# The input gate's tanh stays in its PSUM bank, and the vector engine reads it there half by half

## The chip, the cores and the metric

The kernel runs on one NeuronCore of a Trainium2 chip. The metric is the device time of one execution in microseconds (us); three executions of the kernel before gave 147.38, 147.51 and 147.60, a median of 147.51. Engines are named as the profile names them: PE is the tensor engine's matmuls and PEld its weight loads, DVE the vector engine, ACT the scalar engine, POOL the GpSimd engine, SP the engine that only issues transfers. A differing time of about 0.2% (0.3 us) is the least that such runs tell from no change.

## What is computed

The input x has 16 sequences of 256 tokens with 128 features, 4096 tokens in all. It is layer-normalised to xn, and the output is x + attn(xn) + ffn(xn).

```python
# attn: a gated linear recurrence along each sequence
xc  = causal_depthwise_conv(xn, 4 taps)
r   = sigmoid(xc @ W_r.T + b_r);   i = sigmoid(xc @ W_i.T + b_i)
a   = sigmoid(log_a) ** (8 * r)
h_t = a_t * h_(t-1) + sqrt(1 - a_t^2) * (i_t * xc_t)
attn = rmsnorm(h @ W_out.T) * gamma
# ffn: each token goes to one of 8 experts, at most 512 tokens per expert
e   = argmax(softmax(xn @ Wr));  y = relu(xn @ W1[e]) @ W2[e] * prob[e]
```

A sigmoid is had from a tanh: sigmoid(z) = 0.5 (tanh(z/2) + 1). So `gated` computes (tanh + 1) * xc, and the factor 0.5 is carried in the scale.

## The kernel before, in words

Everything is written out by hand: each engine has its own list of instructions, which it works off in order, and engines wait for one another on counting semaphores (`wait_ge(sem, n)` passes once the count has reached n).

**Stages.** First x is loaded and normalised, the router picks an expert per token, and a table of row numbers per expert is built. Then comes the long middle stage: eight experts one after the other, with the recurrence's work placed between them. At the end the rows of y are loaded back, scaled and added, and the output is stored.

**One expert e** on PE is `turn` (four transposes of the gathered tokens), `up` (12 matmuls into three banks `hbank`) and `down` (16 matmuls, each of which the profile counts twice, x32 on L624). ACT copies the transposed tokens (`columns`, L778), applies the ReLU (`relu`, L786, four times) and rounds the next weights (`lead`, L730). DVE computes the remainders of these roundings (`columns_rest`, L1028, `weights_rest`, L1003) and copies the result out of PSUM (`evict`, L1068; for expert 6 in two halves, L1075; for expert 7 in four quarters, L1080).

**POOL** issues the indirect transfers, one instruction for 128 rows: `gather` (L405) fetches an expert's tokens in four instructions, `scatter` (L417) writes its results in four. Its order is gathers 0 to 3, then scatter 0, gather 4, scatter 1, gather 5, scatter 2, gather 6, scatter 3, gather 7, scatters 4 to 7. A scatter waits for the copies of `evict` on the semaphore `y_done`; the first two instructions of scatter 6 wait for the first half of expert 6, and each instruction of scatter 7 for its own quarter. SP waits for all scatters before it loads the rows of y back (L339).

**The gates.** The tokens of the recurrence are cut into four chunks (c = 0 to 3) of 1024 columns, each of two halves of 512. For a chunk there are four gate halves, i = 0 to 3: i = 0, 1 are the recurrence gate r for the two halves, i = 2, 3 the input gate i. `gate_half(c, i)` on PE (L553 for chunk 0, L561 to L563 for the others) writes into one of two PSUM banks, `gate[i % 2]`; `gate_half` on ACT (L754) applies tanh to it and writes SBUF: `dec` for i = 0, 1 and `inp` for i = 2, 3. ACT's tanh counts up `gate_free`, and PE may write a bank again once the tanh of two gate halves before has read it. So ACT alone frees the gate banks.

**The gated input.** `gated(c)` on DVE (L1045) waits for all four tanhs of the chunk, then computes `inp = (inp + 1) * xc` for both halves from SBUF and counts `gated_done` once. `recur` (L1057, L1061) multiplies it by the scale and runs the recurrence; `project` on PE (L640) multiplies its result by W_out and reuses the gate banks.

**Where these stand in each engine's list.** The plans `PE_AT`, `ACT_AT`, `DVE_AT`, `DVE_LATE` and so on (L294 to L303) place the stages by expert. On PE `gates1` comes behind `down(0)` and ahead of `up(1)`, `gates2` behind `down(1)` and `gates3` behind `down(2)`. On DVE the order from the point of interest is: convolution taps of chunk 2, `columns_rest(1)`, `gated0`, clip 0, `evict(0)`, taps of chunk 3, `split2`, `weights_rest(2)`, `columns_rest(2)`, `gated1`, `evict(1)`, `split3`, clip 1, `gated2`, and so on; `gated3` follows `evict(2)`. On ACT `gates1` is followed by `relu(1)`, `lead2`, `decay1` with its square, and `columns(2)`.

Of the kernel before, what the change touches and what calls it, by code (L numbers as in the profile page):

```python
# [9 lines left out]
ALU = mybir.AluOpType  # L10
# [8 lines left out]
C = 4  # L19
# [27 lines left out]
def rglru_moe_kernel(nc, x, params, gamma, weights, xn_rows, y_rows, out):  # L47
# [17 lines left out]
    with ExitStack() as ctx:  # L65
# [6 lines left out]
        def sem(name):  # L72
            return ctx.enter_context(nc.semaphore(name))
# [163 lines left out]
        clip_done = sem("clip_done")  # L237
        scale_done = sem("scale_done")
        gated_done = sem("gated_done")
        input_done = sem("input_done")  # L240
# [197 lines left out]
        def _(pe):  # L438
# [105 lines left out]
            def gate_half(c, i):  # L544
                n = 4 * c + i
                convolved(pe, 2 * c + i % 2)
                if n >= 2:
                    pe.wait_ge(gate_free, n - 1)
                else:
                    pe.wait_ge(xnT_done, NH)  # L550
# [78 lines left out]
            def project(n):  # L629
# [3 lines left out]
                if n >= 3:  # L633
                    pe.wait_ge(sum_done, n - 2)
                else:
                    pe.wait_ge(gate_free, 4 * C)
                    pe.wait_ge(dump_done, 1)
# [34 lines left out]
        def _(act):  # L672
# [74 lines left out]
            def gate_half(c, i):  # L747
                n = 4 * c + i
                dst, bias = (dec, 0) if i < 2 else (inp, 1)
                act.wait_ge(gate_mm, n + 1)  # L750
                if c == 2 and i == 2:
                    act.wait_ge(low_done, len(LOW_STARTS))
                o = c * TC + (i % 2) * HT
                a(dst[:, o:o + HT], gate[n % 2][:, :], ACT.Tanh, bias=half_b[:, bias:bias + 1],  # L754
                  scale=0.5).then_inc(gate_free, 1)

# [9 lines left out]
            def decay(c):  # L766
                cols = slice(c * TC, (c + 1) * TC)
                if c == 0:
                    act.wait_ge(coef, 6)
                    act.wait_ge(zero_out, 16 * C)  # L770
                act.wait_ge(gate_free, 4 * c + 2)
                a(dec[:, cols], dec[:, cols], ACT.Exp, bias=lna[:, 5:6], scale=lna[:, 5:6]).then_inc(decay_done, 1)
# [81 lines left out]
        def _(dve):  # L854
# [185 lines left out]
            def gated(c):  # L1040
                dve.wait_ge(gate_free, 4 * c + 4)
                convolved(dve, 2 * c)
                convolved(dve, 2 * c + 1)
                for half in halves(c):
                    last = v.scalar_tensor_tensor(inp[:, half], inp[:, half], 1.0, xc[:, half], ALU.add, ALU.mult)  # L1045
                last.then_inc(gated_done, 1)

            def recur(n):
                cols = slice(n * HT, (n + 1) * HT)
                given = obank[IN_OBANK[n]][:, :]  # L1050
                dve.wait_ge(scale_done, n // 2 + 1)
                dve.wait_ge(gated_done, n // 2 + 1)
                if n >= 1:
# [151 lines left out]
```

## Time and profile before

| | |
|---|---|
| median of three executions | 147.51 us |
| span of the profiled execution, first to last instruction | 128.8 us |
| what lies around the span (147.51 less 128.8) | 18.7 us |
| PE busy | 106.2 us, 82% of the span |
| DVE busy | 101.8 us, 79% |
| ACT busy | 99.6 us, 77% |
| POOL busy | 84.6 us, 66% |
| granted TensorE clock, mean over the span | 0.958 of full speed |

The span is that of one profiled execution; no time of its own is given for it beside the span, so the 18.7 us between it and the median are taken as the part outside the first and last instruction. Times in the rows below are microseconds from the span's start. A row of a timeline merges neighbouring instructions of one line (xN); its bracket tells idle time of the engine just before and what ended it. "issue" in the chain of waits, or as a releaser, is time for which the profile shows no one that was waited for. L12 is line 12 of the kernel before.

### The profile page before, as it was taken

Reading aid. Unit: us, or ns where it says so; the run is one execution under the profiler, and the core shown is the slowest. Engines: PE = TensorE matmul, PEld = TensorE weight load, DVE = VectorE, ACT = ScalarE, POOL = GpSimd, SP = SyncE. Lnnn points to the kernel's source line nnn. Section 1 sums busy time; section 2 is a strip of 40 time slices with the busy share of each in tenths; the row PEclk is TensorE's granted clock in tenths of the full one; section 3 lists DMA queues with packets and bytes.
Section 4 is the critical chain, followed back from the end, with each engine's and each line's share of the span. In section 5 each row is a group of like instructions: output and inputs, shape, how many; then the busy total and the mean of one; then the engine's idle time right before and its main releaser. Section 6 shows DMA issues by size and latency. Waiting matters only on the chain.

```text
span 128.8 us, 2229 instructions
## 1 busy us (share of the span) xinstructions
PE 106.2 (82%) x711; PEld 89.9 (70%) x711; DVE 101.8 (79%) x238; ACT 99.6 (77%) x219; POOL 84.6 (66%) x109
## 2 busy tenths in 40 slices
PE   3999999999799999999999997999997999700000
PEld 3999976672379779789879987898697899600000
DVE  5398998999699999979614489999999975973690
ACT  3299792888589589789689999999999799823560
POOL 8987774078788787778777877888787878700000
PEclk9999999999999999999999999999999999998555
DMA  2966964892456365312611711111110111149995
GB/s 85 383 247 173 405 244 173 318 380 66 103 169 181 80 209 139 118 53 56 209 41 41 219 51 41 61 37 41 52 57 25 60 43 61 41 108 302 325 372 215
DMA packets 8234, 19.27 MB, mean 150 GB/s; under 512 B 1689, under 2 KB 1945, under 8 KB 8224
## 3 DMA queue, kind: packets, MB, share of 16 engines
q1 hardware_dynamic: 5424, 13.70, 31.5%
q0 software_dynamic: 2080, 4.19, 11.2%
q10 hardware_dynamic: 720, 1.25, 2.6%
q8 instruction: 5, 0.08, 0.2%
q14 instruction: 5, 0.04, 0.1%
HBM read 10.82 MB, written 8.39 MB: 149 GB/s over the span
## 4 chain that ended last, share of the span: by engine, by line
PE 60%; DVE 9%; DMA 8%; ACT 8%; issue 5%; POOL 4%; POOLq 1%; SPq 1%; DVEq 0%; ACTq 0%
PE bank L624 17%; PE bank L609 6%; PE bank L611 6%; PE bank L610 6%; DMA dec<-y_rows 4%; PE bank L640 4%; PE bank L453 3%; PE bank L561 3%; PE bank L442 3%; POOL xn_tok L405 3%; DMA xn_tok<-xn_rows,idx_in 2%; ACT xc L796 2%; PE bank L594 2%; PE bank L563 2%; PE bank L562 2%
## 5 line engine op out<-in xcount | busy, mean ns | idle before, releaser
L405 POOL DMA_INDIRECT xn_tok<-xn_rows,idx_in x32 | 33.7, 1054 | 14.4 <-issue 9.4
L417 POOL DMA_INDIRECT y_rows<-xn_tok,idx_out x32 | 33.5, 1047 | 9.7 <-issue 9.1
L624 PE MATMUL bank<-w_raw,h_sb 128*128 128x128 f32 x256 | 29.9, 275 | 0.0
L624 PEld LDWEIGHTS bank<-w_raw,h_sb 128*128 128x128 f32 x256 | 29.2, 192 | 0.0
L786 ACT ACTIVATE h_sb<-bank 128x512 f32<-128x512 f32 x32 | 18.8, 598 | 2.5 <-PE bank L611 0.6
L609 PE MATMUL bank<-xg_hi,w_hi 128*128 128x512 f32 x32 | 13.2, 412 | 0.0
L611 PE MATMUL bank<-xg_hi,w_lo 128*128 128x512 f32 x32 | 12.6, 393 | 0.0
L610 PE MATMUL bank<-xg_lo,w_hi 128*128 128x512 f32 x32 | 12.5, 391 | 0.0
L1021 DVE SCALAR_TENSOR_TENSOR xc<-xnT,par,xc 128x1020 f32<-128x1020 f32 (+2 forms) x9 | 11.5, 1277 | 0.3
L640 PE MATMUL bank<-par,xc 128*128 128x128 f32 x64 | 8.8, 280 | 2.2 <-ACT xc L796 1.3
L1061 DVE TENSOR_TENSOR_SCAN xnT<-dec,bank 128x256 f32<-128x256 f32 x16 | 10.1, 674 | 0.3
L640 PEld LDWEIGHTS bank<-par,xc 128*128 128x128 f32 x64 | 8.0, 191 | 3.1 <-ACT xc L796 1.6
L805 ACT ACTIVATE sq<-bank 128x128 f32<-128x128 f32 x32 | 8.9, 277 | 1.0 <-PE bank L640 0.3
L836 ACT ACTIVATE dec<-dec,prob 128x128 f32<-128x128 f32 x16 | 5.1, 389 | 5.8 <-DMA dec<-y_rows 5.8
L380 POOL TENSOR_SCALAR xn_tok<-x_tok,rstd,nmr 128x128 f32<-128x128 f32 x15 | 7.7, 529 | 2.8 <-DVE nmr L884 2.8
L453 PE MATMUL bank<-w_router,dec 128*128 128x128 f32 x64 | 8.6, 278 | 0.4 <-ACT dec L694 0.3
L754 ACT ACTIVATE dec<-bank,half_b 128x512 f32<-128x512 f32 x8 | 5.5, 689 | 4.2 <-PE bank L563 3.2
L453 PEld LDWEIGHTS bank<-w_router,dec 128*128 128x128 f32 x64 | 7.8, 192 | 0.9 <-ACT dec L694 0.5
L1028 DVE TENSOR_TENSOR xg_lo<-bank,xg_hi 128x512 fp32r<-128x512 f32 x8 | 5.5, 688 | 3.5 <-ACT xg_hi L778 3.3
L796 ACT ACTIVATE xc<-xnT 128x512 f32<-128x512 f32 x8 | 8.2, 1105 | 0.0
L609 PEld LDWEIGHTS bank<-xg_hi,w_hi 128*128 128x128 f32 x32 | 6.0, 188 | 2.5 <-DVE xg_lo L1028 0.9
L1045 DVE SCALAR_TENSOR_TENSOR inp<-inp,xc 128x512 f32<-128x512 f32 x8 | 5.2, 689 | 2.9 <-ACT inp L754 2.9
(143 smaller groups left out, 243.2 us busy)
## 6 DMA issues: line engine op xcount, KB each, us to landing
w_raw<-in_weights SPq DMA_DIRECT2D x8, 512.0 KB, 3.9
y_rows<-sca SPq DMA_DIRECT2D x4, 512.0 KB, 5.9
dec<-y_rows SPq DMA_DIRECT2D x8, 256.0 KB, 5.7
x_tok<-in_x SPq DMA_DIRECT2D x3, 512.0 KB, 5.9
xn_rows<-xn_tok SPq DMA_DIRECT2D x3, 512.0 KB, 3.6
out<-dec SPq DMA_DIRECT2D x4, 256.0 KB, 3.1
out<-dec ACTq DMA_DIRECT2D x4, 256.0 KB, 2.9
x_tok<-in_x SPq DMA_DIRECT2D x2, 256.0 KB, 3.5
```

What stands on the lines that cost most here:

```text
L405: g.indirect_dma_start(gathered[:, s * D:(s + 1) * D], None, xn_rows, bass.IndirectOffsetOnAxis(ap=idx_in[:, s:s + 1], axis=0)).then_inc(g ...
L417: g.indirect_dma_start(y_rows, bass.IndirectOffsetOnAxis(ap=idx_out[:, s:s + 1], axis=0), gathered[:, s * D:(s + 1) * D], None, bounds_che ...
L453: last = mm((bank[6], bank[2])[t // PT][:, o:o + D], xT[:, t * P:(t + 1) * P], w_router[:, :], start=True, stop=True)
L609: mm(b, w_hi[:, e % 2, w], xg_hi[:, :], start=True, stop=False)
L610: mm(b, w_hi[:, e % 2, w], xg_lo[:, :], start=False, stop=False)
L611: mm(b, w_lo[:, e % 2, w], xg_hi[:, :], start=False, stop=True).then_inc(h_mm, 1)
L624: last = mm(tile_of(e, s), h_sb[:, k * CAP + s * P:k * CAP + (s + 1) * P], w_raw[:, e, F + k * D:F + (k + 1) * D], start=(k == 0), stop=(k ...
L640: last = mm(obank[n % 3][:, i * D:(i + 1) * D], ordered[:, t * P:(t + 1) * P], par[:, WO_T:WO_T + D], start=True, stop=True)
L786: a(h_sb[:, k * CAP:(k + 1) * CAP], hbank[n % 3][:, :], ACT.Relu).then_inc(h_done, 1)
L796: a(ordered[:, cols].rearrange("d (i p) -> d p i", i=RUN), hs[:, cols].rearrange("d (p i) -> d p i", i=RUN), ACT.Copy).then_inc(order_done, 1)
L1021: ins = v.scalar_tensor_tensor(dst[:, :, back:], src[:, :, 0:L - back], par[:, k:k + 1], dst[:, :, back:], ALU.mult, ALU.add)
L1061: last = v.tensor_tensor_scan(hs[:, o:o + L], dec[:, o:o + L], given[:, s * L:(s + 1) * L], 0.0, ALU.mult, ALU.add)
```

## The change

The semaphore `tanh_done` is new. ACT's tanh of an input-gate half (i = 2, 3) now writes back into the PSUM bank it reads, instead of into `inp`, and counts `tanh_done` instead of `gate_free`. `gated(c)` on DVE now takes the halves one at a time: it waits for that half's tanh, reads it from the PSUM bank `gate[i]`, writes `inp` in SBUF, and counts `gated_done` per half. PE's rule for a gate bank follows: for i = 2, 3 it waits, as before, for the tanh of i - 2 of the same chunk; for i = 0, 1 of a chunk after the first it now waits for `gated` of the chunk before, on that half. `project` waits for both counts, and ACT's wait for `low_done` (the SBUF space of `inp` was shared with a table of the router) is gone, because DVE itself writes `inp` now. The order of the stages on every engine, the number of matmuls, tanhs and DVE operations, and all transfers are as before.

```diff
--- before.py
+++ after.py
@@ -236,6 +236,7 @@
         square_done = sem("square_done")
         clip_done = sem("clip_done")
         scale_done = sem("scale_done")
+        tanh_done = sem("tanh_done")
         gated_done = sem("gated_done")
         input_done = sem("input_done")
         scan_done = sem("scan_done")
@@ -544,8 +545,10 @@
             def gate_half(c, i):
                 n = 4 * c + i
                 convolved(pe, 2 * c + i % 2)
-                if n >= 2:
-                    pe.wait_ge(gate_free, n - 1)
+                if i >= 2:
+                    pe.wait_ge(gate_free, 2 * c + i - 1)
+                elif c >= 1:
+                    pe.wait_ge(gated_done, 2 * (c - 1) + i + 1)
                 else:
                     pe.wait_ge(xnT_done, NH)
                 if c == 0:
@@ -633,7 +636,8 @@
                 if n >= 3:
                     pe.wait_ge(sum_done, n - 2)
                 else:
-                    pe.wait_ge(gate_free, 4 * C)
+                    pe.wait_ge(gate_free, 2 * C)
+                    pe.wait_ge(gated_done, 2 * C)
                     pe.wait_ge(dump_done, 1)
                 for i in range(4):
                     t = 4 * n + i
@@ -746,13 +750,13 @@
 
             def gate_half(c, i):
                 n = 4 * c + i
-                dst, bias = (dec, 0) if i < 2 else (inp, 1)
                 act.wait_ge(gate_mm, n + 1)
-                if c == 2 and i == 2:
-                    act.wait_ge(low_done, len(LOW_STARTS))
-                o = c * TC + (i % 2) * HT
-                a(dst[:, o:o + HT], gate[n % 2][:, :], ACT.Tanh, bias=half_b[:, bias:bias + 1],
-                  scale=0.5).then_inc(gate_free, 1)
+                if i < 2:
+                    o = c * TC + i * HT
+                    a(dec[:, o:o + HT], gate[n % 2][:, :], ACT.Tanh, bias=half_b[:, 0:1], scale=0.5).then_inc(gate_free, 1)
+                else:
+                    a(gate[n % 2][:, :], gate[n % 2][:, :], ACT.Tanh, bias=half_b[:, 1:2],
+                      scale=0.5).then_inc(tanh_done, 1)
 
             def gates(c):
                 for i in range(4):
@@ -768,7 +772,7 @@
                 if c == 0:
                     act.wait_ge(coef, 6)
                     act.wait_ge(zero_out, 16 * C)
-                act.wait_ge(gate_free, 4 * c + 2)
+                act.wait_ge(gate_free, 2 * c + 2)
                 a(dec[:, cols], dec[:, cols], ACT.Exp, bias=lna[:, 5:6], scale=lna[:, 5:6]).then_inc(decay_done, 1)
                 if c < 2:
                     square(c)
@@ -1038,18 +1042,17 @@
                 return [slice(n * HT, (n + 1) * HT) for n in (2 * c, 2 * c + 1)]
 
             def gated(c):
-                dve.wait_ge(gate_free, 4 * c + 4)
-                convolved(dve, 2 * c)
-                convolved(dve, 2 * c + 1)
-                for half in halves(c):
-                    last = v.scalar_tensor_tensor(inp[:, half], inp[:, half], 1.0, xc[:, half], ALU.add, ALU.mult)
-                last.then_inc(gated_done, 1)
+                for i, half in enumerate(halves(c)):
+                    convolved(dve, 2 * c + i)
+                    dve.wait_ge(tanh_done, 2 * c + i + 1)
+                    v.scalar_tensor_tensor(inp[:, half], gate[i][:, :], 1.0, xc[:, half], ALU.add,
+                                           ALU.mult).then_inc(gated_done, 1)
 
             def recur(n):
                 cols = slice(n * HT, (n + 1) * HT)
                 given = obank[IN_OBANK[n]][:, :]
                 dve.wait_ge(scale_done, n // 2 + 1)
-                dve.wait_ge(gated_done, n // 2 + 1)
+                dve.wait_ge(gated_done, 2 * C)
                 if n >= 1:
                     dve.wait_ge(scan_done, n)
                 if n == 6:
```

## Rows read from the trace of the kernel before

**Rows 1.** The page's chain that ended last, by engine:
```profile
PE 60%; DVE 9%; DMA 8%; ACT 8%; issue 5%; POOL 4%; POOLq 1%; SPq 1%; DVEq 0%; ACTq 0%
```

**Rows 2.** The chain of waits, 42 to 82 us: start, duration, engine and line:
```profile
43.26 0.23 PE bank L561
...
44.78 0.47 PE bank L561
...
53.15 0.23 PE bank L561
...
63.05 0.24 PE bank L561
...
75.55 0.25 PE bank L611
...
75.82 0.02 ACT h_sb L786
```

**Rows 3.** POOL's timeline: start, duration, line, operation, idle time before and releaser:
```profile
25.89 0.98 POOL L405 DMA_INDIRECT xn_tok<-xn_rows,idx_in  x1 [4.93 <-DVE idx_out L986]
...
57.97 1.29 POOL L417 DMA_INDIRECT y_rows<-xn_tok,idx_out  x1 [0.30 <-issue]
...
102.41 0.97 POOL L417 DMA_INDIRECT y_rows<-xn_tok,idx_out  x1 [0.31 <-issue]
...
107.52 0.97 POOL L417 DMA_INDIRECT y_rows<-xn_tok,idx_out  x1 [0.30 <-issue]
108.80 0.97 POOL L417 DMA_INDIRECT y_rows<-xn_tok,idx_out  x1 [0.30 <-DVE xn_tok L1080]
...
111.35 0.97 POOL L417 DMA_INDIRECT y_rows<-xn_tok,idx_out  x1 [0.30 <-issue]
```

**Rows 4.** Who waited for whom, POOL: total us, times, longest:
```profile
POOL y_rows L417 <- issue: 9.1, 30, 0.3
```

**Rows 5.** The line of expert 7's copies: duration min/median/max, first and last start:
```profile
L1080 DVE COPY xn_tok<-bank x4: 291/292/292, 105.5 to 108.2; 128x128 f32<-128x128 f32 x4
```

**Rows 6.** DVE's timeline around the couplings to POOL and to ACT:
```profile
24.91 0.19 DVE L985 TENSOR_SCALAR idx_in<-bank 128x32 int32<-128x32 f32 x1 [0.19 <-PE bank L481]
...
79.43 0.69 DVE L1028 TENSOR_TENSOR xg_lo<-bank,xg_hi 128x512 fp32r<-128x512 f32 x1 [0.30 <-ACT xg_hi L778]
...
100.50 0.74 DVE L1075 COPY xn_tok<-bank 128x256 f32<-128x256 f32 x2
...
116.65 1.14 DVE L1168 SCALAR_TENSOR_TENSOR dec<-dec,prob,x_tok 128x128 f32<-128x128 f32 x4 [1.63 <-issue]
```

**Rows 7.** Busy time by stretch: length, PE, PEld, DVE, ACT, POOL, PEclk, DMA share, GB/s:
```profile
79.40:100.50 21.10, 19.53 (x140) 17.41 (x138) 20.18 (x38) 20.14 (x56) 16.53 (x16) 1.00 0.15 45
```

**Rows 8.** DVE's timeline, 43 to 60 us:
```profile
43.09 1.32 DVE L1045 SCALAR_TENSOR_TENSOR inp<-inp,xc 128x512 f32<-128x512 f32 x2
...
53.03 0.69 DVE L1028 TENSOR_TENSOR xg_lo<-bank,xg_hi 128x512 fp32r<-128x512 f32 x1
53.63 1.28 DVE L1045 SCALAR_TENSOR_TENSOR inp<-inp,xc 128x512 f32<-128x512 f32 x2
54.84 0.68 DVE L1068 COPY xn_tok<-bank 128x512 f32<-128x512 f32 x1
...
58.91 1.28 DVE L1045 SCALAR_TENSOR_TENSOR inp<-inp,xc 128x512 f32<-128x512 f32 x2
```

**Rows 9.** ACT's timeline, 43 to 53 us:
```profile
43.99 0.69 ACT L754 ACTIVATE dec<-bank,half_b 128x512 f32<-128x512 f32 x1 [1.31 <-PE bank L563]
...
47.13 2.64 ACT L786 ACTIVATE h_sb<-bank 128x512 f32<-128x512 f32 x4
...
52.42 0.58 ACT L778 ACTIVATE xg_hi<-bank 128x512 fp32r<-128x512 f32 x1
```

**Rows 10.** PE's timeline: the last matmul of `up(1)`:
```profile
48.75 0.39 PE L611 MATMUL bank<-xg_hi,w_lo 128*128 128x512 f32 x1
```

**Rows 11.** DVE's groups by form: count, busy us, mean ns, idle before:
```profile
L1003 DVE TENSOR_TENSOR w_lo<-w_raw,w_hi 128x512 fp32r<-128x512 f32 x8 | 5.5, 689 | 1.9 <-ACT w_hi L730 1.9
L1028 DVE TENSOR_TENSOR xg_lo<-bank,xg_hi 128x512 fp32r<-128x512 f32 x8 | 5.5, 688 | 3.5 <-ACT xg_hi L778 3.3
L1045 DVE SCALAR_TENSOR_TENSOR inp<-inp,xc 128x512 f32<-128x512 f32 x8 | 5.2, 689 | 2.9 <-ACT inp L754 2.9
```

## The prediction

> **What bounds the kernel now.** I read the chain of waits first. By engine it is 60% PE [rows 1], and in its pieces the tensor engine stands in an unbroken string from 43 to 75.8 us: gates, `up`, `turn`, `down`, gates again [rows 2]. At 75.82 it passes to ACT, whose fourth ReLU of expert 4 starts 0.02 us after PE's last `up` matmul ended at 75.80. So in this stretch a microsecond lost on PE is a microsecond lost for PE, ACT and DVE alike.
>
> Then I looked at the end of the chain, because a chain is only as true as its joints. It goes through DVE's last copy of expert 7 to the POOL instruction at 108.80, which the profile puts down to that copy line [rows 3]. But the gap before it is 0.30 us, and 30 of the 32 scatter instructions show the same gap with nobody waited for [rows 4]. The instruction at 108.80 is the second of scatter 7 and needs only the second copy. The four copies start between 105.5 and 108.2 [rows 5], some 0.9 apart, so that one was done near 106.7, two us earlier. POOL was not waiting; it was working off a backlog. From 25.89, when the first gather started, to 112.3 its 64 instructions follow one another with gaps of 0.3 [rows 3, 4]: the train on POOL is a second bound beside PE, and at the end it is the later one. The reader is to take from this that PE's stretch has slack against POOL, and how much is a subtraction:
>
> - scatter 6, first instruction, starts at 102.41 [rows 3]; the first half of `evict(6)` starts at 100.50, and two take 0.74 with the second starting behind the first, so the first ends near 100.91 (100.50 + 0.41) [rows 6];
> - scatter 7, first: 107.52 against a copy that ends at 105.8 [rows 3, 5];
> - scatter 7, last: 111.35 against 108.5;
> - scatter 1: 57.97 against 55.52 (54.84 + 0.68) [rows 3, 8].
>
> What POOL needs between a copy's end and its own start I call L. Its bounds: 0.03, if the constant 0.30 can be spent ahead of the wait (0.03 is what DVE took after ACT's `columns` ended at 79.40 [rows 6]); 0.79, from the index table's copy at 24.91 + 0.19 to the first gather at 25.89 [rows 3, 6]. I take 0.33, the gap of the sixty-odd others plus 0.03. Scatter 6 is the tightest: 102.41 - 0.33 - 100.91 = 1.17 us of slack.
>
> **The change, part by part.** *Two new waits on PE.* Before `gates1` PE needed only ACT's tanhs of chunk 0, done long before; now its first half needs the first half of `gated0`, which DVE starts at 43.09, behind the taps and `columns_rest(1)`. Two halves take 1.32 in all, each 0.68 to 0.69 [rows 8, 11], so the first ends at 43.77 and the second at 44.41. From a release to the matmul PE takes 0.10: the tanh of 43.99 + 0.69 = 44.68 released the matmul at 44.78, and after such a halt the first matmul counts 0.47 in the chain instead of 0.23 [rows 2, 9]. So PE starts at 43.87 and is through its first matmul at 44.34, where it was through at 43.49 (43.26 + 0.23): 0.85 lost. The second half follows under cover: its input is free at 44.41, and PE wants it near 44.8. Behind the halted matmul stand the rest of `gates1`, `up(1)`, `turn(2)`, `down(1)`, and ACT's tanhs and ReLUs wait for those.
>
> Before `gates2` the same wait is on `gated1`. This one starts at 53.63 behind `columns_rest(2)`, which started at 53.03, just after ACT's `columns(2)` ended at 52.42 + 0.58 = 53.00 [rows 8, 9]. Does DVE's side move with PE's? ACT gets to `columns(2)` in order, behind four ReLUs from 47.13 to 49.77, the last of which starts near 49.17; the last `up(1)` matmul ends at 48.75 + 0.39 = 49.14 [rows 9, 10]. So ACT runs at PE's pace, and `gated1` is late by the same 0.85: the first half ends at 53.63 + 0.68 + 0.85 = 55.16, PE starts at 55.26 and is through its first matmul at 55.73, against 53.38 before [rows 2]. That is 2.35 in all: 0.85 from the first wait, 1.50 from the second. Before `gates3` nothing is lost: `gated2` starts at 58.91 and its first half is done by 59.60, PE comes at 63.05 [rows 2, 8], and both move by the same 2.35.
>
> *The tanh written to PSUM.* No ACT write to PSUM stands in the trace. What it could save or cost lies on ACT between the third gate half and `relu`, and there ACT waits for PE matmul by matmul, as shown; a tenth of a microsecond either way per tanh is absorbed within the four ReLUs. I take zero.
>
> *The DVE read from PSUM.* `columns_rest` reads PSUM and takes 688 ns for 128x512, `weights_rest` with SBUF inputs 689, `gated` 689 [rows 11]. I take no difference; the spread of these rows, some 0.02 per half, is the bound, counted once in each of the two waits. Beside this stands a rule that speaks against the change: the Trainium skill (Perfetto Trace Analysis, Optimizing Scalar/DVE Operations) gives a DVE operation an access overhead of about 60 ns on SBUF and about 125 ns on PSUM. By that each of the two waits would grow by an estimated 0.065 us and the forecast below by 0.13, to 148.82; the rows show no such difference.
>
> *Half by half.* `gated3` is the one place where DVE waited for a tanh, 2.9 us once [rows 11]. Its first half can now start one tanh earlier, 0.69; but DVE waits 1.9 for the weights of the next `weights_rest` right after it [rows 11], so this is worth nothing. `recur` now waits for all of `gated`, which stands ahead of it on the same engine anyway. The removed wait for the router's table and the added one in `project` have been satisfied for tens of microseconds. No transfer moves in any queue's order.
>
> *How much reaches the end.* The 2.35 passes over PE and ACT to 79.43, where DVE starts `columns_rest(5)` when ACT releases it, and from there DVE is busy 20.18 of 21.10 us up to `evict(6)` [rows 6, 7], with no wait for another engine that is longer than its own pipeline gaps. So the first half of `evict(6)` ends at 100.91 + 2.35 = 103.26, and scatter 6 starts at 103.59 instead of 102.41: 1.18 late. The train then runs on as before: scatter 7's first would come at 108.70, and its copy is ready at 105.8 + 2.35 + 0.33 = 108.48. The last stage hangs on the last scatter; its DVE work had 1.63 idle before 116.65 [rows 6], more than the 1.17 by which DVE is now later than POOL. So of 2.35 lost on PE, POOL's backlog hides 1.17 and 1.18 reach the end. Against the profiled execution: 128.8 + 1.18 = 129.98; what lies around the span stays, so 147.51 + 1.18 = 148.69.
>
> **The rivals.** *The chain is right as printed* (12%): POOL did wait for the copies, nothing hides, and all 2.35 comes through: 149.86. For it is the releaser named at 108.80; against it the constant gap and the copy finished two us before.
>
> *All of it is hidden, not slower* (13%): the place is POOL before scatter 6, the price saved is the whole loss, and it decides at 1.17: if PE is late by less than that at expert 6, the end doesn't move and the time is 147.51. It needs one wait to fall away, above all the second, when DVE reached `gated1` early enough; then 0.85 is left, under the backlog. For it: the backlog is real in the rows. Against: `columns_rest(2)` started 0.03 after ACT, and ACT 0.03 after PE, so nothing in that string has room. If only the first wait went, 1.50 would be left and 0.33 would show: 147.84.
>
> *The change does not do what it says* would mean that the waits it adds are met on arrival; that is the same time, and DVE's start at 43.09 against PE's at 43.26 speaks against it.
>
> **How the numbers follow.** My forecast has 70%. With L from 0.03 to 0.79 the loss is 0.88 to 1.64, so its own range is 148.4 to 149.2. 3% goes to a gain, 2% to more than 149.9. The range that leaves out under two tenths is 147.7 to 149.9: it drops the hidden case and takes in the full loss. A measurement tells about 0.2%, 0.3 us, from no change: slower 0.84, same 0.13, faster 0.03.
>
> **What would show it.** PE idle about 0.6 us before the first L561 of chunk 1 and 1.3 before that of chunk 2, both released by the DVE line of `gated`, none before chunk 3; `relu`, `columns` and `evict` from expert 2 on later by 2.2 to 2.5; POOL's gaps at 0.3 until scatter 6, and there one real wait of about 1.5 released by `evict`. The forecast is wrong if PE's two halts sum to well under 2, if POOL already waits at an earlier scatter, or if its train ends as early as before.

## The result, and the profile after

The changed kernel takes 149.59 us, median of 20 runs (148.26 to 151.32); the kernel before, run beside it, 148.52 (147.35 to 150.84, 20 runs). The ratio is 1.0107 [1.0081, 1.0133]: slower by about 1%, where the forecast had 1.18 us, 0.80%. The comparison leaves out runs over 1.5% above the fastest of their kernel, which matters here because the kernel before scatters more, and of the six runs each of b0, a0, e2 and y1 below it leaves two. Over all runs the means are 148.82 and 149.66, 0.84 us (0.56%) apart. Two later series gave 1.0009 [0.9888, 1.0129] and 1.0070 [1.0025, 1.0116]; by the means of all their runs it is 1.0016 and 1.0029. So the sign and, roughly, the size are those of the forecast. Its reasons are not, and that the size came near is luck.

The page of the changed kernel (span; the chain's shares by engine, which answer to [rows 1]; POOL's two groups):

```profile
span 146.9 us, 2234 instructions
...
PE 58%; issue 11%; DVE 8%; ACT 6%; DMA 6%; POOL 3%; another core or an unknown queue 3%; POOLq 1%; SPq 1%; DVEq 0%
...
L418 POOL DMA_INDIRECT y_rows<-xn_tok,idx_out x32 | 33.5, 1048 | 29.8 <-DVE xn_tok L1071 15.1
L406 POOL DMA_INDIRECT xn_tok<-xn_rows,idx_in x32 | 32.3, 1010 | 14.4 <-issue 9.4
```

The span is 146.9 us and the time of that execution 148.96: 2.06 us lie around it, where the forecast had 18.7. In every execution of this study that has both on record, whatever the kernel, that difference is 1.7 to 2.5 us. And POOL, which was to have one real wait, at scatter 6, now waits for `evict` at expert after expert. Its waits, which answer to [rows 4] (total us, times, longest):

```profile
POOL y_rows L418 <- DVE xn_tok L1071: 15.1, 5, 3.9
...
POOL y_rows L418 <- issue: 8.2, 25, 0.9
...
POOL y_rows L418 <- DVE xn_tok L1078: 4.9, 1, 4.9
```

The two halts of PE are there: the first in the first row, then all engines of the changed kernel around the second one (start, duration, line, idle time before and its releaser; L564 is the first matmul of a gate half, L1048 `gated`, L756 the tanh of a recurrence half, L1071 `evict`; `remote` is a releaser that the profile can't find among this core's engines and queues). They answer to [rows 2, 8]:

```profile
45.53 0.47 PE L564 MATMUL bank<-xc_hi,wg_hi 128*128 128x512 f32 x1 [1.06 <-issue]
...
60.93 1.28 DVE L1048 SCALAR_TENSOR_TENSOR inp<-bank,xc 128x512 f32<-128x512 f32 x2
61.05 0.95 POOL L406 DMA_INDIRECT xn_tok<-xn_rows,idx_in  x1 [0.30 <-issue]
61.72 0.47 PE L564 MATMUL bank<-xc_hi,wg_hi 128*128 128x512 f32 x1 [1.27 <-issue]
...
63.34 1.27 ACT L756 ACTIVATE dec<-bank,half_b 128x512 f32<-128x512 f32 x2 [3.05 <-PE bank L566]
63.36 0.69 DVE L1071 COPY xn_tok<-bank 128x512 f32<-128x512 f32 x1 [1.15 <-remote]
64.13 0.47 PE L564 MATMUL bank<-xc_hi,wg_hi 128*128 128x512 f32 x1 [0.77 <-issue]
64.85 1.00 POOL L418 DMA_INDIRECT y_rows<-xn_tok,idx_out  x1 [2.85 <-DVE xn_tok L1071]
```

PE is idle 1.27 us before chunk 2, where the forecast said 1.3, and starts 0.11 us after the first half of `gated1` has ended (60.93 + 0.68); before chunk 1 it is idle 1.06 us (0.6 forecast). The last row answers to [rows 3]: a scatter that waits 2.85 us for its copies, where each of those had 0.30. And a surprise stands in the middle: ACT and DVE begin again within 0.02 us of one another, 1.34 us after POOL's last gather instruction ended (61.05 + 0.95). That has no counterpart in the rows ahead of the prediction.

The operations themselves, by form, answer to [rows 11]:

```profile
L758 ACT ACTIVATE bank<-bank,half_b 128x512 f32<-128x512 f32 x8 | 5.3, 662 | 3.2 <-PE bank L566 2.9 <-PE bank L556 0.2
L756 ACT ACTIVATE dec<-bank,half_b 128x512 f32<-128x512 f32 x8 | 5.3, 686 | 11.6 <-PE bank L566 6.4 <-remote 4.2 <-PE bank L556 1.0
...
L1048 DVE SCALAR_TENSOR_TENSOR inp<-bank,xc 128x512 f32<-128x512 f32 x8 | 5.2, 682 | 2.2 <-ACT bank L758 2.2
```

The read from PSUM takes DVE 682 ns (689 from SBUF before), the tanh into PSUM 662 ns (686 into SBUF, the row below it). The 7 ns of DVE are no difference: in z0, one of the runs below, it reads SBUF and takes 682 ns too.

```profile
L1047 DVE SCALAR_TENSOR_TENSOR inp<-inp,xc 128x512 f32<-128x512 f32 x8 | 5.1, 682 | 2.9 <-ACT inp L756 2.9
```

### The profile page after: what moved, and what is told of

It is laid out like the page before. It is cut to its first block, busy times and chain, and to the rows that moved or that the text cites. A ratio compares the mean times of both kernels' runs of the same rounds, so it can differ in the third digit from the quotient of the medians.

```text
span 146.9 us, 2234 instructions
## 1 busy us (share of the span) xinstructions
PE 114.0 (78%) x711; PEld 94.9 (65%) x711; DVE 102.2 (70%) x238; ACT 99.2 (68%) x219; POOL 83.2 (57%) x109
## 4 chain that ended last, share of the span: by engine, by line
PE 58%; issue 11%; DVE 8%; ACT 6%; DMA 6%; POOL 3%; another core or an unknown queue 3%; POOLq 1%; SPq 1%; DVEq 0%
PE bank L627 15%; PE bank L612 6%; PE bank L614 6%; PE bank L613 6%; PE bank L644 4%; DMA dec<-y_rows 3%; PE bank L564 3%; PE bank L566 3%; PE bank L565 3%; PE bank L454 3%; PE bank L443 2%; POOL xn_tok L406 2%; PE bank L597 2%; PE bank L508 2%
## 5 line engine op out<-in xcount | busy, mean ns | idle before, releaser
L406 POOL DMA_INDIRECT xn_tok<-xn_rows,idx_in x32 | 32.3, 1010 | 14.4 <-issue 9.4
L627 PE MATMUL bank<-w_raw,h_sb 128*128 128x128 f32 x256 | 30.9, 276 | 2.5 <-issue 2.5
L790 ACT ACTIVATE h_sb<-bank 128x512 f32<-128x512 f32 x32 | 18.7, 598 | 6.8 <-PE bank L614 3.0
L612 PE MATMUL bank<-xg_hi,w_hi 128*128 128x512 f32 x32 | 14.4, 449 | 0.8 <-ACT h_sb L790 0.8
L613 PE MATMUL bank<-xg_lo,w_hi 128*128 128x512 f32 x32 | 13.7, 429 | 0.0
L614 PE MATMUL bank<-xg_hi,w_lo 128*128 128x512 f32 x32 | 13.6, 425 | 0.0
L756 ACT ACTIVATE dec<-bank,half_b 128x512 f32<-128x512 f32 x8 | 5.3, 686 | 11.6 <-PE bank L566 6.4
L1071 DVE COPY xn_tok<-bank 128x512 f32<-128x512 f32 x6 | 4.1, 688 | 10.1 <-remote 9.6
L564 PE MATMUL bank<-xc_hi,wg_hi 128*128 128x512 f32 x12 | 5.9, 495 | 6.5 <-issue 6.4
L612 PEld LDWEIGHTS bank<-xg_hi,w_hi 128*128 128x128 f32 x32 | 7.2, 224 | 3.3 <-ACT h_sb L790 1.4
L782 ACT ACTIVATE xg_hi<-bank 128x512 fp32r<-128x512 f32 x8 | 4.7, 587 | 6.2 <-remote 5.7
L564 PEld LDWEIGHTS bank<-xc_hi,wg_hi 128*128 128x128 f32 x12 | 2.6, 215 | 9.6 <-issue 9.3
```

Of the source, the lines that this page charges most:

```text
L406: g.indirect_dma_start(gathered[:, s * D:(s + 1) * D], None, xn_rows, bass.IndirectOffsetOnAxis(ap=idx_in[:, s:s + 1], axis=0)).then_inc(g ...
L564: mm(gate[n % 2][:, :], wg_hi[:, w], xc_hi[:, half], start=True, stop=False)
L612: mm(b, w_hi[:, e % 2, w], xg_hi[:, :], start=True, stop=False)
L613: mm(b, w_hi[:, e % 2, w], xg_lo[:, :], start=False, stop=False)
L614: mm(b, w_lo[:, e % 2, w], xg_hi[:, :], start=False, stop=True).then_inc(h_mm, 1)
L627: last = mm(tile_of(e, s), h_sb[:, k * CAP + s * P:k * CAP + (s + 1) * P], w_raw[:, e, F + k * D:F + (k + 1) * D], start=(k == 0), stop=(k ...
```

## The experiments

Theory A is the forecast. Theory B: the timed executions are not like the profile it rested on; they hold standstills inside the span (stretches of a microsecond and more in which PE, ACT and DVE all stand), POOL has no backlog, and PE's new waits fall into these standstills. All ratios are to the kernel before, run on the same chip in the same series.

| run | median us (runs) | ratio [95%] |
|---|---|---|
| b0_before | 151.33 (6) | 0.9965 [0.9872, 1.0057] |
| a0_after, a1_after | 150.28 (6), 151.00 (12) | 1.0009 [0.9888, 1.0129], 1.0070 [1.0025, 1.0116] |
| e1_gated_earlier | 151.19 (6) | 1.0143 [1.0076, 1.0210] |
| e2_waits_only | 151.68 (6) | 0.9995 [0.9905, 1.0085] |
| x1_gated_later | 151.21 (6) | 1.0101 [1.0034, 1.0168] |
| y3_third_bank | 151.19 (6) | 1.0153 [1.0083, 1.0223] |
| x2_pool_longer | 149.36 (12) | 0.9925 [0.9871, 0.9978] |
| x3_gathers_first | 162.10 (6) | 1.0828 [1.0759, 1.0897] |
| y1_spaced | 147.90 (6) | 0.9883 [0.9803, 0.9962] |
| y2_direct | 138.76 (6) | 0.9360 [0.9323, 0.9398] |
| z0_direct_again | 139.24 (6) | 0.9368 [0.9284, 0.9452] |
| z1_direct_after | 140.44 (6) | 0.9432 [0.9350, 0.9514] |
| z2_direct_third | 138.94 (6) | 0.9329 [0.9257, 0.9401] |
| y4_after_longer | 149.44 (12) | 0.9995 [0.9933, 1.0057] |
| y5_third_longer | 146.22 (6) | 0.9862 [0.9817, 0.9906] |
| w1_ahead3 | 150.18 (12) | 1.0045 [0.9990, 1.0100] |
| w2_third_ahead3 | 148.82 (12) | 0.9999 [0.9960, 1.0038] |

**Is the first profile like the timed runs?** The kernel before, unchanged, and the changed one, unchanged.

> The kernel before, unchanged, profiled again. The first profile had a span of 128.8 us against timed runs of 147.5, the changed kernel's has 146.9 against 148.96. Theory A (the forecast: the new waits on PE, part of them hidden by POOL's backlog; the 18.7 us lie outside the span): span again near 129, POOL without waits. Theory B (the timed runs hold pauses that the first profile did not have, so POOL has no backlog in them): span near 145, with POOL waiting for evict at several experts. The ratio to the kernel before is 1.000 by both, and its interval says what can be told.

> The changed kernel, unchanged, on the same chip as the other runs of this set. Both theories: 1.007 to 1.013 of the kernel before. The profile says whether the long pauses seen in its first profile (ACT and DVE idle together for 2 to 4 us near 46, 74 and 103 us) come at the same places again; Theory B expects pauses of the same total, Theory A expects them to be an accident of one execution.

POOL's waits in the kernel before, profiled again in an execution of 151.31 us (the first line has the span):

```profile
core 0 of [0], span 149.4 us
...
POOL y_rows L417 <- DVE xn_tok L1068: 15.0, 5, 3.2
...
POOL y_rows L417 <- issue: 8.1, 25, 0.8
...
POOL y_rows L417 <- DVE xn_tok L1075: 4.9, 1, 4.9
```

Set against [rows 4] this is another execution of the same code: a span of 149.4 instead of 128.8, and the waits for `evict` that the changed kernel has too. They are no effect of the change. The same place as above, in this trace:

```profile
56.19 3.74 PE L624 MATMUL bank<-w_raw,h_sb 128*128 128x128 f32 x32
...
59.68 0.48 PE L561 MATMUL bank<-xc_hi,wg_hi 128*128 128x512 f32 x1
...
60.23 0.40 PE L563 MATMUL bank<-xc_hi,wg_lo 128*128 128x512 f32 x1
...
60.41 1.32 DVE L1045 SCALAR_TENSOR_TENSOR inp<-inp,xc 128x512 f32<-128x512 f32 x2
...
61.66 0.95 POOL L405 DMA_INDIRECT xn_tok<-xn_rows,idx_in  x1 [0.30 <-issue]
64.04 1.27 ACT L754 ACTIVATE dec<-bank,half_b 128x512 f32<-128x512 f32 x2 [4.27 <-remote]
64.06 0.69 DVE L1068 COPY xn_tok<-bank 128x512 f32<-128x512 f32 x1 [2.33 <-remote]
64.83 0.47 PE L561 MATMUL bank<-xc_hi,wg_hi 128*128 128x512 f32 x1 [3.51 <-issue]
```

PE begins chunk 2's gates at 59.68 without a wait and has two halves ready by 61.3, but ACT doesn't take them up before 64.04. PE then stands 3.51 us. By the code ACT's tanh waits for the count of the first of these halves, whose last matmul ended at 60.63, and `evict(1)` for that of `down(1)`, which ended at 59.93; PE's third half waits for the tanh. So PE's work is done, and what it hands on is taken up 3.4 us late by ACT and 2.3 us late by DVE, which is free from 61.73 on; no wait that the kernel asks for explains it. In the changed kernel PE comes to the same two halves 2 us later (61.72), and ACT takes them up at 63.34: 1.34 us after POOL's last gather there, 1.43 us here. So the 1.27 us of the second wait lie inside a standstill of both kernels. Of the 20.6 us between the two spans, 0.9 arise ahead of POOL's first gather (26.82 against 25.89 [rows 3]), 8.3 from there to `evict(1)` (64.06 against 54.84 [rows 8]), 9.9 from there to `evict(6)` (55.5 against 45.7 [rows 6, 8]) and 1.5 behind it. A slower PE is part of the standstills' price. The same trace by stretches (length, busy time and instructions of PE, PEld, DVE, ACT and POOL, granted clock, DMA share, GB/s):

```profile
46.00:49.00 3.00, 1.01 (x3) 0.75 (x4) 1.28 (x2) 0.88 (x1) 2.11 (x2) 0.99 0.49 182
49.20:52.20 3.00, 2.87 (x6) 1.66 (x6) 2.10 (x3) 1.38 (x2) 0.55 (x1) 0.50 0.44 105
```

While PE stands, from 46 to 49 us, the granted clock is still full; then it is 0.50, the lower of its two levels (1.2 of 2.4 GHz), and a gate matmul that took 0.39 us takes 0.63. In the first trace the clock is full until 118 us.

> The changed kernel once more, unchanged, for the size of the effect. Theory A: 1.18 us slower than the kernel before, ratio 1.008. Theory B (the new waits fall into pauses): ratio 1.000 plus or minus 0.003 as far as the scatter of the runs can tell, and a span some 2 us below the time.

Its ratio, 1.0070, is the second sign that the change costs something although the waits are covered, a weak one, as its 1.0029 over all runs says. In the traces the standstills lie in the same places: `evict(0)` to `evict(3)` start at 50.1, 64.1, 77.2 and 90.3 us in a0, at 49.8, 63.8, 77.0 and 90.1 in a1, and at 50.1, 64.1, 77.2 and 90.3 in the kernel before (b0). The forecast had `evict` later by 2.2 to 2.5 us from expert 2 on; `evict(2)` and `evict(3)` show nothing of it.

**PE's waits in the kernel as it is.** Four edits shift, add, lengthen or remove them.

e1, on the changed kernel: `gated0` ahead of `columns_rest(1)`, `gated1` behind `split2`.

> The changed kernel, with gated0 and gated1 moved ahead on DVE: gated0 in front of columns_rest(1), gated1 behind split2, so that PE finds the first half of each done when it comes. Theory A (the two waits are the loss): PE's halts before gates1 and gates2 fall from 0.6 and 1.3 us to under 0.2, and the time returns to the kernel before, ratio 0.998 to 1.002. Rival (the loss comes from the PSUM accesses or from elsewhere): the time stays where the changed kernel is, 1.007 to 1.013.

In its trace PE comes to both chunks without idle time (45.52 and 59.65), and the time doesn't return: 1.0143.

e2, on the kernel before: PE waits as in the changed kernel, the tanh still goes through SBUF.

```diff
+                    if c >= 1 and i < 2:
+                        pe.wait_ge(gated_done, 2 * (c - 1) + i + 1)
```

> The kernel before, tanh through SBUF as it was, but PE's first two gate halves of a chunk also wait for gated of the chunk before, half by half: the new waits without the PSUM accesses. Theory A: as slow as the changed kernel, 1.007 to 1.013 of the kernel before. Rival (PSUM accesses): no slower than before, 0.998 to 1.002.

The halts are there without the change, 0.68 us before chunk 1 and 1.42 before chunk 2, and here the profile names `gated` as what ended the second:

```profile
62.68 0.47 PE L563 MATMUL bank<-xc_hi,wg_hi 128*128 128x512 f32 x1 [1.42 <-DVE inp L1047]
```

x1, on the changed kernel: `gated` behind `evict`.

```diff
-        DVE_AT = {0: "gated0 clip0", 1: "gated1", ...
-        DVE_LATE = {0: "taps3 split2", 1: "split3 clip1 gated2", ...
+        DVE_AT = {0: "clip0", ...
+        DVE_LATE = {0: "gated0 taps3 split2", 1: "gated1 split3 clip1 gated2", ...
```

> The changed kernel with gated of chunk 0 moved behind evict(0) and gated of chunk 1 behind evict(1) on the vector engine, so that the tensor engine's two new waits last longer (by the first trace evict(0) ends at 55.5 and evict(1) some ten later, where the tensor engine wants the banks at 43.3 and 53.2). Theory A (the waits run into the end, less a backlog of 1.2 us on POOL): several us lost at each of the two halts, at least 2.7 us (1.9%) beyond the kernel before, ratio 1.019 or more. Theory B (the timed executions hold pauses of 1.5 to 3 us in every expert, in which PE, ACT and DVE stand anyway, and the wait for POOL's gathers comes last there): ratio to the kernel before 1.00 to 1.01, as the changed kernel itself.

Its first halt is seven times that of the changed kernel, and `evict(1)` comes when it came before (63.67; 64.06 in the kernel before profiled again):

```profile
50.69 0.76 PE L564 MATMUL bank<-xc_hi,wg_hi 128*128 128x512 f32 x1 [7.18 <-issue]
...
63.67 0.68 DVE L1071 COPY xn_tok<-bank 128x512 f32<-128x512 f32 x1
```

The time is 1.0101, that of the changed kernel, where theory A asked for 1.019 or more: A fails here. y3 takes the waits away with a third bank:

```diff
-        gate = [bank[4], bank[5]]
+        gate = [bank[4], bank[5], bank[7]]
...
-                if i >= 2:
-                    pe.wait_ge(gate_free, 2 * c + i - 1)
+                if i == 3:
+                    pe.wait_ge(gate_free, 2 * c + 1)
+                elif c >= 1 and i == 0:
+                    pe.wait_ge(gate_free, 2 * c)
...
+                    pe.wait_ge(gated_done, 2 * (c - 1) + i)
```

> The changed kernel with three gate banks used in turn (4, 5 and 7) instead of two, so that PE needs a bank that gated still reads one half later: by the first trace neither new wait is left over 0.1 us. The tanh to PSUM and the read by DVE from PSUM stay. Theory A (the change costs through PE's waits): as fast as the kernel before, ratio 1.000. Theory C (it costs by what DVE and ACT do on PSUM, not by the waits): as the changed kernel, 1.007 to 1.010. Theory B (the change costs nothing that these runs can tell): 1.000, as A.

1.0153: taking the waits away brought nothing back, nor did e1, and adding them alone (e2, 0.9995) cost nothing that could be told, though its interval reaches to 1.0085. Against the forecast's 0.8% the intervals, some 0.7 to 0.9% to either side, are wide; what the four say together is that the time of this kernel doesn't visibly follow PE's waits. By themselves e1 and y3 would fit theory C; z2 below speaks against it.

**Where do the standstills come from?** x2 makes POOL slower, x3 gives it all gathers at a stretch.

```diff
                 if e + AHEAD < E:
+                    g.iota(low_eq[:, e * P // 4:(e + 1) * P // 4, :], [[1, P // 4], [0, NT]], base=0,
+                           channel_multiplier=0, **exact)
                     gather(e + AHEAD)
```

> The kernel before with one more instruction on POOL (an iota of about 1.1 us into a table that nobody reads any more) between scatter(e) and gather(e+4) for e = 0 to 3. Theory A (POOL has a backlog at scatter 6 of the trace, so what delays POOL delays the end): up to 4.6 us more at the end (3%), 1.03, with POOL's waits for evict only at the last expert. Theory B (POOL waits for evict at five to eight experts, some 20 us in all, and evict in turn resumes 1 to 2 us after POOL's last gather instruction): evict(1) to evict(4) come later by up to 1.1 us each, 2 to 4.6 us in all (1.3 to 3%), and POOL's waits stay as they are. If POOL's waits only absorb the addition, with PE setting the pace: no change, ratio 1.00, and POOL's waits shorter by 4.6 us.

```diff
-            AHEAD = 4
+            AHEAD = 8
```

> The kernel before with POOL issuing all eight gathers ahead of scatter 0 (before: four). Theory A (POOL is busy from the first gather to the last scatter without a wait): the same 64 instructions in another order, the scatters' train ends at the same place, ratio 0.99 to 1.01. Theory B (the three engines' pauses hang on the alternation of POOL's gathers and evict): the pauses at experts 1 to 4 go or move, POOL's waits for evict of some 20 us shrink, and the time falls by 2 to 10 us (1.3 to 7%). If the pauses come from POOL's instructions being under way at all, whatever their order: they come earlier, the sum stays, ratio 1.00.

Both went another way than either theory had it. 4.7 us more work on POOL made the kernel faster, 0.9925. All gathers first made it 8% slower. The timeline of x3:

```profile
39.95 3.98 PE L624 MATMUL bank<-w_raw,h_sb 128*128 128x128 f32 x32
...
46.51 0.40 PE L563 MATMUL bank<-xc_hi,wg_lo 128*128 128x512 f32 x1 [0.94 <-issue]
...
48.74 0.63 PE L563 MATMUL bank<-xc_hi,wg_lo 128*128 128x512 f32 x1
...
66.94 0.95 POOL L405 DMA_INDIRECT xn_tok<-xn_rows,idx_in  x1 [0.30 <-issue]
72.08 1.27 ACT L754 ACTIVATE dec<-bank,half_b 128x512 f32<-128x512 f32 x2 [26.30 <-remote]
72.10 0.69 DVE L1068 COPY xn_tok<-bank 128x512 f32<-128x512 f32 x1 [25.60 <-remote]
...
72.87 0.77 PE L561 MATMUL bank<-xc_hi,wg_hi 128*128 128x512 f32 x1 [23.50 <-issue]
```

From 49.4 to 72.1 PE, ACT and DVE do nothing, and all POOL does in that time is issue gathers. They go on 4.2 us after its last one. Again ACT and DVE wait for counts of PE, and the matmuls behind these ended at 46.91 (the first gate half) and 43.93 (`down(0)`). So B holds as to the place and failed as to the direction: not the alternation of gathers and `evict` makes the standstills, the longer train without a break makes the longer one. y1 loosens the train, y2 takes half of the gathers off POOL.

```diff
+            def pause(n):
+                g.iota(low_eq[:, 4 * n:4 * n + 4, :], [[1, 4], [0, NT]], base=0, channel_multiplier=0, **exact)
...
+                    if e >= AHEAD:
+                        pause(s - AHEAD * ST + (e - AHEAD + 1) * ST)
...
+                    if e < E - AHEAD:
+                        pause(s + e * ST)
```

> The kernel before with a short iota (128 elements a partition, a few tenths of a us) on POOL behind each of the 32 instructions of scatters 0 to 3 and gathers 4 to 7, so that its indirect transfers follow less densely. Theory A (POOL has a backlog and the end hangs on it): some 10 us and more later, ratio 1.07 or above. Theory B (POOL waits for evict for some 20 us in all, and the standstills of PE, ACT and DVE come with dense trains of indirect transfers): the standstills between 45 and 100 us get shorter, POOL's waits for evict take the additions, ratio 0.98 to 1.00.

```diff
-                if e + AHEAD < E:
-                    gather(e + AHEAD)
...
+                if e >= 4:
+                    sp.wait_ge(xn_tp, e + 1)
+                    for s in range(ST):
+                        sp.dma_start(tiles(xn_tok, e * ST + s, 1), own_rows(xn_rows, e * ST + s, 1)).then_inc(gather_in[e], 16)
```

> The kernel before with gathers 4 to 7 left to SP as plain transfers of 512 rows an expert in four parts (the wrong rows, so what experts 4 to 7 compute is another thing, of the same size), and no gather on POOL behind the first four. Theory A (the same work of PE, ACT and DVE, 18.7 us outside the span): POOL's backlog goes and the end comes up to 2 us earlier, ratio 0.985 to 1.00, standstills unchanged. Theory B (the standstills come with POOL's train of indirect transfers): from 50 us on PE, ACT and DVE run as in the first trace, evict(1) to evict(4) follow one another at about 10 us instead of 13 to 14, and the time falls by 8 to 15 us (ratio 0.90 to 0.95).

y1: 0.9883 (0.988 by the means of all runs too), with 9.4 us more work on POOL (32 iotas of 293 ns). y2: 0.9360, as B had it. DVE's timeline in y2, `evict(1)`, and the line of `evict(6)`'s two halves (duration min/median/max, first and last start):

```profile
61.40 0.69 DVE L1070 COPY xn_tok<-bank 128x512 f32<-128x512 f32 x1
```

```profile
L1077 DVE COPY xn_tok<-bank x2: 416/416/417, 107.0 to 107.4; 128x256 f32<-128x256 f32 x2
```

45.6 us from the one to the other: the first trace has 45.7 (54.84 to 100.50 [rows 6, 8]), the second trace of the kernel before 55.5. With POOL's gathers gone from that stretch the standstills are gone from it, to a tenth of a microsecond. y2 takes away POOL's issuing and the indirect transfers together; which of the two it is stays untested.

w1 shortens the first train by one gather (`AHEAD = 3`).

> The kernel before with POOL issuing three gathers ahead of scatter 0 (before: four). Theory A: the same 64 instructions in another order, ratio 0.99 to 1.01. Theory B (a standstill ends 1 to 2 us after an uninterrupted train of indirect transfers does, and does not begin in its first 15 us or so): the first train ends near 43 instead of 48, the standstill at 45 to 50 goes, evict(0) starts near 46 instead of 50, and the time falls by 2 to 4 us (1.3 to 2.7%), unless the next train, which is as long as before, takes it back.

`evict(0)` comes at 46.9 instead of 50.1, as B had it, but `evict(5)` at 110.3 instead of 109.6: the later trains take it all back, 1.0045.

```profile
46.86 0.68 DVE L1068 COPY xn_tok<-bank 128x512 f32<-128x512 f32 x1
...
110.28 0.69 DVE L1068 COPY xn_tok<-bank 128x512 f32<-128x512 f32 x1 [7.46 <-remote]
```

**The waits where no standstill covers them.** z0 is y2 again; z1 and z2 have the same edit on the changed kernel, with two and with three gate banks.

> The kernel of y2_direct once more, unchanged (the kernel before with gathers 4 to 7 as plain transfers of SP, wrong rows for experts 4 to 7), as the base for the next two. Every theory: 0.932 to 0.940 of the kernel before, some 139 us, span 2 to 3 us less.

> The changed kernel with the same edit as z0 (plain transfers for gathers 4 to 7). In y2's trace PE reaches the first matmul of chunk 2's gates at 59.47 and the first half of gated1 ends near 60.20 + 0.68 = 60.88. Theory A as far as it concerns PE (a wait that nothing covers costs what it lasts): PE idle 1.5 us there, evict(2) and all after it 1.5 us later than in z0, time 1.5 us (1.1%) above z0, since POOL has no backlog to hide it; the first wait, at 44.6, is covered by the standstill at 45 to 50. Theory C (the cost is in what DVE and ACT do on PSUM): the loss builds up over all chunks, also at chunk 3. Theory B's strong form (the change costs nothing at all): within 0.3% of z0.

> The changed kernel with three gate banks in turn and the same edit as z0. Theory A: PE comes to a bank that gated has left by 0.1 us at worst, so no loss, within 0.3% of z0. Theory C: as z1, 1.1% above z0.

The start of `gated1`, PE's first matmul of chunk 2 and `evict(2)`, first in z0, then z1, then z2:

```profile
60.47 0.48 PE L563 MATMUL bank<-xc_hi,wg_hi 128*128 128x512 f32 x1
61.20 1.28 DVE L1047 SCALAR_TENSOR_TENSOR inp<-inp,xc 128x512 f32<-128x512 f32 x2
...
70.98 0.68 DVE L1070 COPY xn_tok<-bank 128x512 f32<-128x512 f32 x1
```

```profile
60.71 1.28 DVE L1050 SCALAR_TENSOR_TENSOR inp<-bank,xc 128x512 f32<-128x512 f32 x2
61.49 0.47 PE L566 MATMUL bank<-xc_hi,wg_hi 128*128 128x512 f32 x1 [1.27 <-issue]
...
71.95 0.68 DVE L1073 COPY xn_tok<-bank 128x512 f32<-128x512 f32 x1
```

```profile
60.13 0.48 PE L570 MATMUL bank<-xc_hi,wg_hi 128*128 128x512 f32 x1
60.86 1.28 DVE L1054 SCALAR_TENSOR_TENSOR inp<-bank,xc 128x512 f32<-128x512 f32 x2
61.64 0.47 PE L570 MATMUL bank<-xc_hi,wg_hi 128*128 128x512 f32 x1 [0.56 <-issue]
...
71.01 0.68 DVE L1077 COPY xn_tok<-bank 128x512 f32<-128x512 f32 x1
```

From the start of `gated1` to `evict(2)` it takes 9.78 us in z0, 11.24 in z1, 10.15 in z2. The wait costs 1.46 (the forecast's 1.50), and the third bank gives 1.09 of it back (0.56 us of a wait is left one half later, where the expectation had 0.1). In z1 the later stages keep the delay: `evict(2)` to the first half of `evict(6)` is 37.1 us in both. By the trace's clock it is 0.97 us at `evict(2)`, because z1 came to `gated1` 0.49 earlier, and 0.99 where SP starts to load the rows of y (123.23 against 122.24); the loads and stores behind that differ by as much the other way, so that these two executions took the same 139.25 us. Over all runs z1 is 1.20 us above z0 by medians (0.86 by means, with a standard error of 0.5 from the six runs each) and 1.50 above z2: the times agree with the wait's price, and it is the traces that show it. The read from PSUM and the work half by half cost nothing that can be told: z2 is not above z0.

**Versions.** The changed kernel with x2's iota, with two banks and with three, and the latter with `AHEAD = 3`.

> The changed kernel, two gate banks, with the iota of 1.1 us on POOL ahead of each of gathers 4 to 7. If the waits cost 0.7 to 1% and the looser train gains 0.75%, each by itself: ratio to the kernel before 1.000, and 1.0 to 1.4% above y5, which has three banks. If the third bank gives nothing: 0.986, as y5.

> The changed kernel with three gate banks, and with the iota of 1.1 us on POOL ahead of each of gathers 4 to 7 that made the kernel before 0.75% faster. If both reasons hold (PE's waits cost the change its 0.7 to 1%, and a looser train on POOL gives 0.75%): ratio to the kernel before 0.990 to 0.995, faster than either kernel. If the iota's gain was chance: 1.000. If the change costs elsewhere: 1.00.

> The changed kernel with three gate banks, three gathers ahead of scatter 0, and the iota of 1.1 us between scatter and gather of experts 0 to 3. If the gains of y5 and of the shorter first train add up: ratio to the kernel before 0.96 to 0.975. If the standstills only move: 0.985, as y5.

y5 is faster than both kernels, 0.9862, with y1 (the kernel before, spaced) beside it at 0.9883. y4 against x2 is the change once more, 0.9995 to 0.9925: 0.7%, from two series whose intervals overlap. The shorter first train added to y5 loses its gain, 0.9999, where 0.96 to 0.985 was expected.

## Why the prediction was wrong

The size was near by luck, by way of a sum whose second half doesn't belong to the executions that were timed: it halved the two waits by a backlog that isn't there, and what covers them is something the forecast didn't know of. The step that failed is "what lies around the span stays, so 147.51 + 1.18", and with it the backlog of 1.17 us that was read from that span: 18.7 us were taken to lie outside the first and last instruction. 2 us do. The other 17 are inside the span, and the traces of these executions show standstills there. Nothing in [rows 1 to 11] shows them, but the subtraction in the table did: a part outside the span of 13% of the time was a number to doubt, and it was carried on as a constant.

- *The new waits on PE, 0.85 and 1.50.* Right as mechanism. The second lasts 1.27 us in the changed kernel and costs 1.46 where nothing covers it (z1 against z0). The first is 1.06, and PE then stutters through the first standstill, until DVE goes on at 49.5 (50.1 in the kernel before), so that it costs nothing that is seen. None before chunk 3, apart from a standstill. The path from there to the end failed: `evict` is not later from expert 2 on.
- *POOL's backlog of 1.17 us at scatter 6.* Wrong for the timed executions: POOL waits there at five experts and more, about 20 us in all. "POOL already waits at an earlier scatter" was named as a sign against the forecast, and it is what the profile after shows. What hides the second wait is the standstill that ends 1.34 and 1.43 us after POOL's last gather in the two kernels. One more term was mis-sized: where POOL does wait, it starts 0.77 to 0.90 us after the copy has ended (65.56 against 64.06 + 0.69 above), not L = 0.33; with 0.81 the same sum would have lost 1.66 us.
- *The rival that all is hidden* named POOL before scatter 6 as the place. The covering is real, in another place, and it isn't complete: the change costs 0.6 to 1.1%.
- *The tanh written to PSUM and the read from it, at zero.* Right: 662 and 682 ns, and z2 is no slower than z0. By the Trainium skill (Perfetto Trace Analysis, Optimizing Scalar/DVE Operations) the DVE read would be an estimated 65 ns longer from PSUM; the rows show no difference, 682 ns from either. That ACT writes PSUM faster than SBUF, as the Trainium skill has it (ScalarE: Activation LUTs, Step-by-step: what each stage is for), agrees with 662 against 686 ns.
- *"A measurement tells about 0.2%, 0.3 us"* came from three runs within 0.22 us. Twenty runs of the kernel before lie between 147.35 and 150.84, so one microsecond is hard to tell in a series of six.

What stays open is how the 1.5 us that the wait is worth become the 0.8 to 1.6 us (0.56 to 1.07%) that are measured in the unaltered kernel. That a part of it is not covered is argued, not shown: x1's longer waits didn't cost more, and y3, which takes them away, was not faster, while y5 against y4 and z2 against z1 were. The times scatter from run to run (those of the kernel before have a standard deviation of 1.2 to 1.6 us), and single traces can't place one microsecond among the standstills.

## What to carry to other kernels

Before trusting a trace, compare its span with the timed median: where they differ by more than the microseconds of start and end (1.7 to 2.5 here), profile again, because the trace may be of an execution unlike those that are timed. A wait is worth what it lasts only in a stretch in which nothing else stands; to price it, take the standstill out of the kernel and measure the wait there. And a train of indirect transfers can be too dense for the other engines: a short pause on POOL, which has time to spare, was worth about as much (0.75 to 1.2%) as the change under study costs (0.6 to 1.1%).

## What the runs showed of the hardware

PE, ACT and DVE stop together while POOL issues indirect transfers without a break. In the second trace of the kernel before the first late start comes 12 us into the first train: ACT's fourth ReLU of expert 0 starts at 41.22, 2.2 us after the matmul that it waits for has ended (38.98). Some 18 us into the train (26.8 to 45 us with four gathers, 26.3 to 45 with eight) PE begins to stutter, even between the matmuls of one accumulation, which wait for no semaphore. ACT and DVE stand at waits for counts of PE whose matmuls have ended, while a count of ACT is passed on promptly in the same stretch: DVE starts `columns_rest(1)` at 44.69, 0.03 us after ACT's `columns(1)`. They go on together after the train's last instruction, 1.1 to 1.7 us in the kernel before and 4.2 us in x3. POOL's own instructions keep their 0.95 us and 0.30 us gaps through the stop of x3, which lasted 22.7 us with eight gathers at a stretch.

The same train ran without any stop in the first trace. What differs between the two kinds of execution isn't shown. One trait goes with it: the first trace holds 2519 semaphore records, the second of the same kernel 1684, and where transfers land is missing in part. The loss lies within POOL's train alone: ahead of its first gather the two traces hold 460 and 454 records, behind its last scatter 578 and 629, in between 1481 and 601. The Trainium skill (NOTIFIC — the notification-queue block, Overflow: three behaviours, one of which stalls the engine) says that the unit that writes such records holds up its producers rather than lose records inside, and that a full queue in memory can drop them. The one would fit the stops, the other the lost records, but no run here shows either. The executions timed here were recorded too, so it is open whether the standstills belong to the kernel alone or to its being recorded.
